# A selective scan and a quantized layer on eight cores: four of a tile's 16 states, in place of three, go without DMA transposes

## The chip, the cores and the metric

The program runs on the 8 cores of one Trainium2 chip. The input has 4 sequences of 2048 positions and 4096 channels. Core c takes one half (1024 positions) of sequence c // 2. The cores exchange nothing: a core that has a second half works out for itself the state in which the first half ends. All cores run the same instructions. The metric is the device time of the slowest core in microseconds (us), lower is better; the time given is the median over runs.

## The reference

With D = 4096 channels, N = 16 states for each channel, and C, B and dt computed from x:

```python
A = -exp(A_log)
xp = einsum('bld,rd->blr', x, x_proj_w)           # gives dt_in (128), B (16), C (16)
dt = softplus(einsum('blr,dr->bld', dt_in, dt_proj_w) + dt_proj_b)
h[t] = exp(dt[t] * A) * h[t-1] + dt[t] * B[t] * x[t]   # for each channel and each of 16 states
y[t] = sum_n(h[t, n] * C[t, n]) + D * x[t]
x = layernorm(x + y)
x = layernorm(x + ffn(x))    # ffn: 4096 x 4096, rows and weights rounded to 8 bits, product rescaled
```

## The kernel before

It has three stages. First the projection of x to dt_in, B and C. Then the scan, in 32 tiles of 128 channels with 16 states each, which are 512 states `g`; the change is here. Last the quantized layer and the second normalization. `L981` and the like are lines of the kernel; PE is TensorE, DVE is VectorE, ACT is ScalarE, POOL is GpSimd, SP is SyncE, whose queue issues the transfers of the scan.

**The scan of one state.** Channels lie on partitions, 1024 positions on the free axis. ACT makes the decay `dAr` (L727). PE makes the input `ps_I` (L505): the transposed `uT` (dt times x) against a diagonal matrix of B, 8 matmuls. DVE scans `hr = dAr * h + ps_I` (L981). Then C must be multiplied in and the 16 states summed into `ps_y`. An ordinary state does it through a DMA transpose: SP turns `hr` to `hT` (L340, `turn_h`), and PE multiplies a diagonal matrix of C by `hT` (L539). A state in `ZN` does it without: POOL multiplies `hr` by a replicated C (`gz`, L1199, `times_C`), and PE adds it in with an identity matrix (L530).

**The state that is carried in.** The first half of the sequence (the prefix) gives only its last state. ACT makes decays `Er` of it (L718). An ordinary state: POOL weighs `wr = Er * up` (L1188, `weigh`), SP turns it to `wT` (L334, `turn_w`), PE sums against a column of B into `ps_c` (L469). DVE copies the finished sums of the whole tile to `carry` in one instruction (L960, `take_carry`), which the scans of the next tile wait for. A state in `ZN`: PE multiplies the transposed `upT` by a diagonal matrix into one of the two `ps_I` buffers (L492), and DVE multiplies and sums it with the decay `Ez` in one instruction (L947, `last_state_z`). So it needs neither `wr` nor `wT`.

**The order.** Every engine's order is written out. All loop over g; the part of the loop with g % 16 = n is called slot n here. In slot n

- DVE does `last_state_z` if the state 18 ahead is in `ZN` (before the change in slots 2, 7 and 12), then the scan of state n; after slot 8's scan the reversed sum of dt (L915, its first operand is `ones`), after slot 10's scan `dD` (L953), after slot 13's scan `take_carry`;
- ACT makes the decay `dAr` for 3 states ahead, once the scan of the slot before is over, then `Er` or `Ez` for 21 states ahead, then pieces of dt;
- POOL does `times_C` if state n - 1 is in `ZN`, then `weigh` for 21 states ahead (nothing if that one is in `ZN`), and at the end of slot 4 `up` (L1167), of slot 6 `uo` (L1174), of slot 7 the cast of x (L1179);
- SP issues `turn_w` for 21 states ahead, which waits for POOL, then `turn_h` for state n, and behind these `yT_st` and `xp` in slot 6, `upT` in slot 7, `uT` in slot 8, `xo` in slot 9;
- PE fills `ps_I` for slot n + 1 (the prefix group first, if that slot has one), then sums `ps_c` for 18 states ahead, then adds states into `ps_y`, most of them three slots after their scan; states 0 and 1 are added in slot 5, behind the evacuation of the tile before (L734).

The last state of a tile that goes into `carry`, number 15, is weighed and turned in slot 10. Ring sizes: `hr` 5, `hT` 6, `wr` 4, `wT` 5, `ps_I` 2, `Er` 3, `Ez` 2, `gz` 2. A scan waits until the state five before it has been turned or multiplied by C.

Of the kernel before, what the change touches and what calls it, by code (L numbers as in the profile page):

```python
# [8 lines left out]
BF16 = mybir.dt.bfloat16  # L9
# [9 lines left out]
def _build(D, P, L, N, R):  # L19
# [10 lines left out]
    nc = bass.Bass("TRN2", target_bir_lowering=False)  # L30
# [16 lines left out]

    c_hbm = nc.dram_tensor("c_st", [3, L], BF16).ap()
    yT_hbm = nc.dram_tensor("yT_st", [L, D], BF16).ap()
# [4 lines left out]
    with es:  # L54
# [88 lines left out]
        esD = ExitStack()  # L143
        BT = sb(esD, "BT", 2 * NC8 * 32, BF16)
        diagB = sb(esD, "diagB", N * NC8 * 128, BF16)
        diagC = sb(esD, "diagC", N * NC8 * 128, BF16)
        ones = sb(esD, "ones", P, BF16)
        xp, xo = sb(esD, "xp", P), sb(esD, "xo", L)
# [6 lines left out]
        uo = sb(esD, "uo", L, BF16)  # L155
        Crep = sb(esD, "Crep", 3 * L, BF16)
        gz = [sb(esD, f"gz{k}", L, BF16) for k in range(2)]
# [10 lines left out]
        carry = sb(esD, "carry", 2 * N)  # L168
        carryZ = sb(esD, "carryZ", 2 * 3)
        yTs = sb(esD, "yTs", 2 * L, BF16)  # L170
# [42 lines left out]
        def nz(k):  # L213

            return 3 * (k // N) + sum(1 for z in ZN if z < k % N)

# [49 lines left out]
        def _(sp):  # L266
# [39 lines left out]

            sp.wait_ge(l_cst, 48)
            sp.dma_start(out=Crep[:], in_=bass.AP(c_hbm.tensor, 0, [[0, 128], [1, 3 * L]])).then_inc(l_C, 16)

# [10 lines left out]
            def turn_up(i):  # L320
                sp.wait_ge(g_up, i + 1)
                if i >= 2:
                    sp.wait_ge(p_P, 3 * (i - 1))
                sp.dma_start(out=by_piece(upT[i % 2]), in_=up[i % 2][:], transpose=True).then_inc(l_up, 16)
# [559 lines left out]
        def _(v):  # L884
# [26 lines left out]
            def reverse_sum(i):  # L911

                v.wait_ge(a_ln, 2 * i + 1)
                v.wait_ge(g_up, i + 1)
                nc.vector.tensor_tensor_scan(dtp[i % 2][:], ones[:], dtp[i % 2][:], tot[i % 2][:],  # L915
                                             OP.mult, OP.subtract).then_inc(v_R, 1)
# [22 lines left out]
            def last_state_z(p):  # L939
                i, n = divmod(p, N)  # L940
                o = (i % 2) * 3 + ZN.index(n)
                v.wait_ge(a_E, p + 1)
                v.wait_ge(p_P, nz(p) + 1)
                if i >= 2:
                    v.wait_ge(v_O, N * (i - 2) + n + 1)
                E = Ez[nz(p) % 2]
                nc.vector.scalar_tensor_tensor(E[:], E[:], 1.0, ps_I[place[("P", p)] % 2][:],  # L947
                                               OP.mult, OP.mult, accum_out=carryZ[:, o : o + 1]).then_inc(v_P, 1)
# [13 lines left out]
            def scan(g):  # L962
# [191 lines left out]
        def _(g_):  # L1154
# [35 lines left out]
            def times_C(g):  # L1190
# [125 lines left out]
```

## Time and profile before

| | |
|---|---|
| three runs | 2585.11, 2590.03, 2603.1 us; median 2590.03 |
| profiled execution | 2607.06 us in all; span of its slowest core 2605.5 us |
| spans of the 8 cores | 2585.2 to 2605.5 us |
| first scan to last scan in the profile | about 202 to 1832 us |
| busy share of the span | DVE 72%, PE 63%, ACT 62%, POOL 54% |

The trace is of the slowest core in one execution. In its timelines each row is a start, a duration, the engine, the line, the operation, the tiles, a count, and in brackets how long the engine was idle before it and what it then got. An "x2" stands for two instructions in a row. Instructions that follow each other directly overlap a little in these rows, so two scans take 4.58 us and not twice 2.33. A row of an SP issue is the time that the queue took for it, not the transfer; how long it takes until data lands is in the table of issues. The DMA share of a stretch is a mean over 16 engines and can exceed 1.

### The profile page before, as it was taken

The numbers are of one execution on the slowest core, as the hardware profiler recorded it, in microseconds if no ns is written. First come the engines' busy times: TensorE is split into PE (matmuls) and PEld (weight loads), VectorE is DVE, ScalarE is ACT, GpSimd is POOL, SyncE is SP. The second block draws the span as 40 slices with busy tenths as digits, with TensorE's granted clock in tenths as the row PEclk, the third lists the DMA queues.
The fourth block names the chain that finished last, engine by engine and source line by source line (L and its number), as shares of the span: only waits on it lengthen the run. The fifth ranks groups of instructions, "written<-read, shape, count | busy, mean of one in ns | idle before, by whom it ended". The sixth has DMA issues, their size and how long they took to land.

```text
span 2605.5 us, 47762 instructions; the slowest of 8 cores (2585.2 to 2605.5 us)
## 1 busy us (share of the span) xinstructions
PE 1641.3 (63%) x16180; PEld 1242.0 (48%) x16304; DVE 1885.6 (72%) x1375; ACT 1611.1 (62%) x1603; POOL 1395.0 (54%) x733
## 2 busy tenths in 40 slices
PE   4615566666666656666666656566134579999993
PEld 1114555555555555655555555556023345555541
DVE  1188888888888988888888888889464545555543
ACT  2356777787777777877787777776255444444420
POOL 0027788778877877887788778874112101111110
PEclk8956666666666666666666666767557789999997
DMA  9868999999998999999999999998877445656559
GB/s 312 283 121 139 166 158 174 172 165 164 185 172 155 176 168 172 156 177 172 164 163 173 179 165 157 180 172 134 267 283 246 184 155 201 201 195 202 195 205 339
DMA packets 1014787, 491.47 MB, mean 189 GB/s; under 512 B 984723, under 2 KB 984851, under 8 KB 1000982
## 3 DMA queue, kind: packets, MB, share of 16 engines
q1 hardware_dynamic: 998326, 360.48, 72.6%
q10 hardware_dynamic: 5472, 79.69, 8.7%
q0 software_dynamic: 10752, 48.24, 5.6%
q8 instruction: 136, 2.23, 0.4%
q14 instruction: 101, 0.83, 0.2%
HBM read 196.77 MB, written 56.63 MB: 97 GB/s over the span
## 4 chain that ended last, share of the span: by engine, by line
PE 23%; SPq 22%; DMA 17%; DVE 14%; issue 10%; POOL 8%; ACT 5%; another core or an unknown queue 1%; DVEq 0%; ACTq 0%; POOLq 0%
PE ps_F L615 15%; SPq L340 10%; DVE hr L981 8%; SPq L334 8%; DMA hT<-hr 5%; POOL wr L1188 4%; DMA xld<-xT 4%; DMA ye<-yT_st 4%; PE ps_y L539 2%; PE ps_T L598 2%; POOL up L1167 2%; DMA wT<-wr 2%; PE ps_I L505 2%; ACT Er L718 2%; POOL gz L1199 1%
## 5 line engine op out<-in xcount | busy, mean ns | idle before, releaser
L1188 POOL TENSOR_TENSOR wr<-Er,up 128x1024 bf16<-128x1024 bf16 x399 | 855.4, 2147 | 340.4 <-ACT Er L718 328.5
L981 DVE TENSOR_TENSOR_SCAN hr<-dAr,carry,ps_I 128x1024 bf16<-128x1024 bf16 x416 | 960.1, 2332 | 65.8 <-PE ps_I L505 63.8
L727 ACT ACTIVATE dAr<-dto,A_sb 128x1024 bf16<-128x1024 f32 x512 | 585.7, 1145 | 371.6 <-DVE hr L981 367.3
L505 PE MATMUL ps_I<-diagB,uT 128*128 128x128 bf16 x4096 | 439.7, 271 | 230.8 <-DVE hr L981 223.3
L539 PE MATMUL ps_y<-hT,diagC 128*128 128x128 bf16 x3328 | 354.9, 277 | 224.3 <-DMA hT<-hr 224.0
L505 PEld LDWEIGHTS ps_I<-diagB,uT 128*128 128x128 bf16 x4096 | 357.1, 125 | 266.8 <-issue 264.6
L718 ACT ACTIVATE Er<-dtp,A_sb 128x1024 bf16<-128x1024 f32 x416 | 471.5, 1135 | 15.6 <-DVE wr L937 9.3
L615 PE MATMUL ps_F<-slab,xqT 128*128 128x512 bf16 x1989 | 452.0, 382 | 5.0 <-issue 1.1
L539 PEld LDWEIGHTS ps_y<-hT,diagC 128*128 128x128 bf16 x3328 | 285.2, 126 | 244.1 <-issue 243.7
L615 PEld LDWEIGHTS ps_F<-slab,xqT 128*128 128x128 bf16 x2048 | 200.4, 99 | 234.6 <-issue 9.8
L469 PE MATMUL ps_c<-BT,wT 128*128 128x1 bf16 x3328 | 146.1, 166 | 170.8 <-DMA wT<-wr 150.6
L469 PEld LDWEIGHTS ps_c<-BT,wT 128*128 128x128 bf16 x3328 | 136.5, 105 | 198.3 <-issue 197.1
L1199 POOL TENSOR_TENSOR gz<-hr,Crep 128x1024 bf16<-128x1024 bf16 x96 | 203.9, 2124 | 50.0 <-DVE hr L981 49.7
L981 DVE TENSOR_TENSOR_SCAN hr<-dAr,carryZ,ps_I 128x1024 bf16<-128x1024 bf16 x96 | 223.4, 2327 | 4.4 <-issue 0.5
L1068 DVE SCALAR_TENSOR_TENSOR o<-ps_F,asc,wscR 128x512 f16<-128x512 f32 x64 | 48.0, 751 | 209.7 <-PE ps_F L615 209.6
L1234 POOL DMA_DIRECT2D dch<-d_st x64 | 35.3, 551 | 299.3 <-DMA r_st<-dch 205.6
L825 ACT ACTIVATE sqj<-dch 128x512 bf16<-128x512 f32 x56 | 35.3, 630 | 253.1 <-DVE dch L1082 253.1
L947 DVE SCALAR_TENSOR_TENSOR Ez<-Ez,ps_I 128x1024 bf16<-128x1024 bf16 x96 | 116.8, 1217 | 100.9 <-PE ps_I L492 100.6
L1036 DVE TENSOR_REDUCE wamax<-Wn 128x1 f32<-128x4096 f32 x32 | 141.1, 4410 | 2.0 <-DMA Wn<-W 2.0
L1167 POOL TENSOR_TENSOR up<-dtp,xp 128x1024 bf16<-128x1024 f32 x32 | 75.9, 2371 | 112.4 <-DMA xp<-xT 101.3
L587 PE MATMUL ps_T<-identh_sb,qb 128*128 128x128 f16 x256 | 29.4, 302 | 143.7 <-ACT qb L781 91.1
L788 ACT ACTIVATE qb<-Wn,wqs 128x4096 f16<-128x4096 f32 x32 | 118.3, 3698 | 0.0
(94 smaller groups left out, 1899.9 us busy)
## 6 DMA issues: line engine op xcount, KB each, us to landing
Wn<-W ACTq DMA_DIRECT2D x30, 2048.0 KB, 9.6
xld<-xT SPq DMA_DIRECT2D x32, 1024.0 KB, 11.3
xp<-xT SPq DMA_DIRECT2D x32, 512.0 KB, 5.5
xo<-xT SPq DMA_DIRECT2D x32, 512.0 KB, 5.1
slab<-x_own SPq DMA_DIRECT2D x8, 2048.0 KB, 12.2
d_st<-slab POOLq DMA_DIRECT2D x8, 2048.0 KB, 13.3
dch<-d_st POOLq DMA_DIRECT2D x64, 256.0 KB, 3.6
r_st<-dch POOLq DMA_DIRECT2D x56, 256.0 KB, 3.7
```

Of the source, the lines that this page charges most:

```text
L334: sp.dma_start(out=by_piece(wT[k % 5]), in_=wr[k % 4][:], transpose=True).then_inc(l_w[k % 5], 16)
L340: sp.dma_start(out=by_piece(hT[g % 6]), in_=hr[g % 5][:], transpose=True).then_inc(l_h[g % 6], 16)
L469: mm = pe.matmul(ps_c[:, o : o + 1], wT[k % 5][:, c * 128 : (c + 1) * 128], BT[:, c * 32 + n : c * 32 + n + 1], start=(c == 0), stop=(c == ...
L505: mm = pe.matmul(ps[:, c * 128 : (c + 1) * 128], uT[i % 2][:, c * 128 : (c + 1) * 128], diagB[:, o : o + 128], start=True, stop=True)
L539: mm = pe.matmul(ps_y[:, c * 128 : (c + 1) * 128], diagC[:, o : o + 128], hT[g % 6][:, c * 128 : (c + 1) * 128], start=False, stop=(n == N ...
L615: mm = pe.matmul(ps_F[q % 5][:], xqT[:, kt * L + tt * 128 : kt * L + (tt + 1) * 128], slab[jg % 2][:, kt * 512 : (kt + 1) * 512], start=(k ...
L718: act.activation(dst[:], dtp[i % 2][:], AF.Exp, scale=A_sb[:, p : p + 1]).then_inc(a_E, 1)
L727: act.activation(dAr[g % 4][:], dto[i % 3][:], AF.Exp, scale=A_sb[:, g : g + 1]).then_inc(a_dA, 1)
L981: nc.vector.tensor_tensor_scan(hr[g % 5][:], dAr[g % 4][:], ps_I[place[("O", g)] % 2][:], first, OP.mult, OP.add).then_inc(v_O, 1)
L1036: v.reduce_max(wamax[:, b : b + 1], Wn[b % 2][:], axis=AX.X, apply_absolute_value=True).then_inc(v_wam, 1)
L1188: g_.tensor_tensor(wr[k % 4][:], Er[k % 3][:], up[i % 2][:], OP.mult).then_inc(g_w, 1)
L1199: g_.tensor_tensor(gz[z % 2][:], hr[g % 5][:], Crep[:, o : o + L], OP.mult).then_inc(g_c, 1)
```

## The change

States 2, 6, 10 and 14 of each tile go the way without transposes, in place of 4, 9 and 14. For room in SBUF `ones` shrinks from 1024 columns to 16, and the reversed sum reads its first element with a step of 0.

```diff
-    c_hbm = nc.dram_tensor("c_st", [3, L], BF16).ap()
+    c_hbm = nc.dram_tensor("c_st", [4, L], BF16).ap()
...
-        ones = sb(esD, "ones", P, BF16)
+        ones = sb(esD, "ones", 16, BF16)
...
-        Crep = sb(esD, "Crep", 3 * L, BF16)
+        Crep = sb(esD, "Crep", 4 * L, BF16)
...
-        carryZ = sb(esD, "carryZ", 2 * 3)
+        carryZ = sb(esD, "carryZ", 2 * 4)
...
-        ZN = (4, 9, 14)
+        ZN = (2, 6, 10, 14)
...
-            return 3 * (k // N) + sum(1 for z in ZN if z < k % N)
+            return 4 * (k // N) + sum(1 for z in ZN if z < k % N)
...
-            sp.wait_ge(l_cst, 48)
-            sp.dma_start(out=Crep[:], in_=bass.AP(c_hbm.tensor, 0, [[0, 128], [1, 3 * L]])).then_inc(l_C, 16)
+            sp.wait_ge(l_cst, 64)
+            sp.dma_start(out=Crep[:], in_=bass.AP(c_hbm.tensor, 0, [[0, 128], [1, 4 * L]])).then_inc(l_C, 16)
...
-                nc.vector.tensor_tensor_scan(dtp[i % 2][:], ones[:], dtp[i % 2][:], tot[i % 2][:],
+                nc.vector.tensor_tensor_scan(dtp[i % 2][:], bass.AP(ones, 0, [[16, 128], [0, P]]), dtp[i % 2][:], tot[i % 2][:],
...
-            for it in diag_order[:3]:
+            for it in diag_order[:4]:
...
-            left = diag_order[3:]
+            left = diag_order[4:]
...
-                    g_.wait_ge(p_y, (z - 2) // 3 * N + ZN[(z - 2) % 3] + 1)
+                    g_.wait_ge(p_y, (z - 2) // 4 * N + ZN[(z - 2) % 4] + 1)
...
-                o = (z % 3) * L
+                o = (z % 4) * L
```


In each tile there are two transposes fewer (12 `wT`, 12 `hT`, `upT` and `uT`, where there were 13 and 13), one `weigh` fewer and one `times_C` more on POOL, and one more L947 on DVE. `last_state_z` now stands in slots 0, 4, 8 and 12; slots 1, 5, 9 and 13 have no `wr` and no `wT`, slots 2, 6, 10 and 14 no `hT`.

SP's queue from the `wT` of slot 6 to that of slot 10, before (ahead of it stand `wT` and `hT` of slot 5):

```order
L334 DMA_TRANSPOSE wT<-wr 128x8x128
L340 DMA_TRANSPOSE hT<-hr 128x8x128
L344 DMA yT_st<-yTs 128x8x128
L297 DMA xp<-xT 128x1024
L334 DMA_TRANSPOSE wT<-wr 128x8x128
L340 DMA_TRANSPOSE hT<-hr 128x8x128
L324 DMA_TRANSPOSE upT<-up 128x8x128
L334 DMA_TRANSPOSE wT<-wr 128x8x128
L340 DMA_TRANSPOSE hT<-hr 128x8x128
L318 DMA_TRANSPOSE uT<-uo 128x8x128
L302 DMA xo<-xT 128x1024
L334 DMA_TRANSPOSE wT<-wr 128x8x128
```

The same changed, from the `wT` of slot 6 (ahead of it stands the `hT` of slot 5, which has no `wT` now) to those of slots 10 and 11:

```order
L334 DMA_TRANSPOSE wT<-wr 128x8x128
L344 DMA yT_st<-yTs 128x8x128
L297 DMA xp<-xT 128x1024
L334 DMA_TRANSPOSE wT<-wr 128x8x128
L340 DMA_TRANSPOSE hT<-hr 128x8x128
L324 DMA_TRANSPOSE upT<-up 128x8x128
L334 DMA_TRANSPOSE wT<-wr 128x8x128
L340 DMA_TRANSPOSE hT<-hr 128x8x128
L318 DMA_TRANSPOSE uT<-uo 128x8x128
L340 DMA_TRANSPOSE hT<-hr 128x8x128
L302 DMA xo<-xT 128x1024
L334 DMA_TRANSPOSE wT<-wr 128x8x128 x2
```

Slot 6 has no `hT` any more, slot 9 has one, and between the `wT` of slot 7 and that of slot 10 there stand 7 transfers where there were 6.

POOL in slots 4 to 8 before (the first row is slot 4's `up`; its four rows with `wr` belong to slots 5, 6, 7 and 8):

```order
L1167 TENSOR_TENSOR up1<-dtp1,xp 128x1024
L1199 TENSOR_TENSOR gz1<-hr0,Crep 128x1024
L1188 TENSOR_TENSOR wr2<-Er1,up0 128x1024
L1188 TENSOR_TENSOR wr3<-Er2,up0 128x1024
L1174 TENSOR_TENSOR uo<-dto2,xo 128x1024
L1188 TENSOR_TENSOR wr0<-Er0,up0 128x1024
L1179 CAST x160<-xo 128x1024
L1188 TENSOR_TENSOR wr1<-Er1,up0 128x1024
```

The same changed, from slot 3's `gz` to slot 8's `wr`:

```order
L1199 TENSOR_TENSOR gz0<-hr3,Crep 128x1024
L1188 TENSOR_TENSOR wr2<-Er0,up0 128x1024
L1188 TENSOR_TENSOR wr3<-Er1,up0 128x1024
L1167 TENSOR_TENSOR up1<-dtp1,xp 128x1024
L1188 TENSOR_TENSOR wr0<-Er2,up0 128x1024
L1174 TENSOR_TENSOR uo<-dto2,xo 128x1024
L1199 TENSOR_TENSOR gz1<-hr2,Crep 128x1024
L1188 TENSOR_TENSOR wr1<-Er0,up0 128x1024
L1179 CAST x160<-xo 128x1024
L1188 TENSOR_TENSOR wr2<-Er1,up0 128x1024
```

`gz` moved out of slot 5 into slots 3 and 7, and slot 4 has a `wr`, in front of `up`. In slot 7 a `gz` stands ahead of the `wr`.

DVE from slot 12 (its L947) to slot 2 of the next tile, before; the row L960 is `take_carry`:

```order
L947 SCALAR_TENSOR_TENSOR Ez0,carryZ<-Ez0,ps_I0 128x1024
L981 SCALAR_TENSOR_TENSOR hr3<-dAr0,carry,ps_I1 128x1024
L981 SCALAR_TENSOR_TENSOR hr4<-dAr1,carry,ps_I0 128x1024
L960 COPY carry<-ps_c 128x16
L981 SCALAR_TENSOR_TENSOR hr0<-dAr2,carryZ,ps_I1 128x1024
L981 SCALAR_TENSOR_TENSOR hr1<-dAr3,carry,ps_I0 128x1024
L981 SCALAR_TENSOR_TENSOR hr2<-dAr0,carry,ps_I1 128x1024
L981 SCALAR_TENSOR_TENSOR hr3<-dAr1,carry,ps_I0 128x1024
L947 SCALAR_TENSOR_TENSOR Ez1,carryZ<-Ez1,ps_I1 128x1024
```

The same changed, from slot 12 to slot 1:

```order
L947 SCALAR_TENSOR_TENSOR Ez1,carryZ<-Ez1,ps_I1 128x1024
L981 SCALAR_TENSOR_TENSOR hr3<-dAr0,carry,ps_I0 128x1024
L981 SCALAR_TENSOR_TENSOR hr4<-dAr1,carry,ps_I1 128x1024
L960 COPY carry<-ps_c 128x16
L981 SCALAR_TENSOR_TENSOR hr0<-dAr2,carryZ,ps_I0 128x1024
L981 SCALAR_TENSOR_TENSOR hr1<-dAr3,carry,ps_I1 128x1024
L947 SCALAR_TENSOR_TENSOR Ez0,carryZ<-Ez0,ps_I0 128x1024
L981 SCALAR_TENSOR_TENSOR hr2<-dAr0,carry,ps_I1 128x1024
L981 SCALAR_TENSOR_TENSOR hr3<-dAr1,carry,ps_I0 128x1024
```

Behind `take_carry` the L947 of slot 2 now stands two scans earlier, in slot 0.

## Rows read from the trace of the kernel before

**Rows 1.** The page: span and cores, transfer rate in 40 slices, HBM traffic.

```profile
span 2605.5 us, 47762 instructions; the slowest of 8 cores (2585.2 to 2605.5 us)
...
GB/s 312 283 121 139 166 158 174 172 165 164 185 172 155 176 168 172 156 177 172 164 163 173 179 165 157 180 172 134 267 283 246 184 155 201 201 195 202 195 205 339
...
HBM read 196.77 MB, written 56.63 MB: 97 GB/s over the span
```

**Rows 2.** Busy time by stretch: the 30 middle tiles, then 4.5 us inside one.

```profile
core 2: us, PE busy (x) PEld busy (x) DVE busy (x) ACT busy (x) POOL busy (x), PEclk, DMA share, GB/s
210.50:1761.40 1550.90, 960.43 (x11819) 870.94 (x11878) 1324.69 (x751) 1186.94 (x1197) 1238.63 (x571) 0.66 1.00 168
1049.00:1053.50 4.50, 4.50 (x42) 4.22 (x41) 2.61 (x2) 4.50 (x6) 4.36 (x4) 0.50 0.46 88
```

**Rows 3.** Waits of VectorE over the same 30 tiles: total us, times, longest.

```profile
engine line waited for: us in total, times, longest us
DVE Ez L947 <- PE ps_I L492: 98.8, 70, 3.4
DVE hr L981 <- PE ps_I L505: 63.6, 85, 3.1
DVE carry L960 <- PE ps_c L469: 57.5, 30, 3.7
```

**Rows 4.** Timeline of VectorE over one tile and into the next.

```profile
1039.81 4.58 DVE L981 TENSOR_TENSOR_SCAN hr<-dAr,carry,ps_I 128x1024 bf16<-128x1024 bf16 x2
...
1052.99 1.22 DVE L947 SCALAR_TENSOR_TENSOR Ez<-Ez,ps_I 128x1024 bf16<-128x1024 bf16 x1 [1.89 <-PE ps_I L492]
...
1069.92 1.22 DVE L947 SCALAR_TENSOR_TENSOR Ez<-Ez,ps_I 128x1024 bf16<-128x1024 bf16 x1 [0.55 <-PE ps_I L492]
...
1074.18 2.35 DVE L981 TENSOR_TENSOR_SCAN hr<-dAr,carry,ps_I 128x1024 bf16<-128x1024 bf16 x1 [0.77 <-PE ps_I L505]
1078.11 0.17 DVE L960 COPY carry<-ps_c 128x16 f32<-128x16 f32 x1 [1.58 <-PE ps_c L469]
...
1085.18 4.58 DVE L981 TENSOR_TENSOR_SCAN hr<-dAr,carry,ps_I 128x1024 bf16<-128x1024 bf16 x2 [2.17 <-PE ps_I L505]
1090.33 1.22 DVE L947 SCALAR_TENSOR_TENSOR Ez<-Ez,ps_I 128x1024 bf16<-128x1024 bf16 x1 [0.57 <-PE ps_I L492]
...
1091.47 4.58 DVE L981 TENSOR_TENSOR_SCAN hr<-dAr,carry,ps_I 128x1024 bf16<-128x1024 bf16 x2
```

**Rows 5.** Timeline of SP's queue in the same tile: the issues of transfers.

```profile
1053.38 1.23 SPq L334 DMA_TRANSPOSE wT<-wr  x1
...
1059.76 1.92 SPq L297 DMA_DIRECT2D xp<-xT  x1
1061.84 1.25 SPq L334 DMA_TRANSPOSE wT<-wr  x1
...
1071.43 0.52 SPq L302 DMA_DIRECT2D xo<-xT  x1
1072.11 1.24 SPq L334 DMA_TRANSPOSE wT<-wr  x1
```

**Rows 6.** Timeline of GpSimd in the same tile.

```profile
1044.64 2.12 POOL L1188 TENSOR_TENSOR wr<-Er,up 128x1024 bf16<-128x1024 bf16 x1 [1.77 <-ACT Er L718]
1046.72 2.36 POOL L1167 TENSOR_TENSOR up<-dtp,xp 128x1024 bf16<-128x1024 f32 x1
...
1055.47 2.37 POOL L1174 TENSOR_TENSOR uo<-dto,xo 128x1024 bf16<-128x1024 f32 x1
1057.79 2.13 POOL L1188 TENSOR_TENSOR wr<-Er,up 128x1024 bf16<-128x1024 bf16 x1
```

**Rows 7.** Timeline of ScalarE there: slot 4's and slot 6's prefix decay.

```profile
1046.42 1.13 ACT L718 ACTIVATE Ez<-dtp,A_sb 128x1024 bf16<-128x1024 f32 x1
...
1052.05 1.14 ACT L718 ACTIVATE Er<-dtp,A_sb 128x1024 bf16<-128x1024 f32 x1
```

**Rows 8.** Timeline of TensorE there: three groups that had waited.

```profile
1048.81 1.01 PE L525 MATMUL ps_y<-dD,x 128*128 128x128 bf16 x8 [0.84 <-ACT yTs L734]
...
1077.60 0.34 PE L469 MATMUL ps_c<-BT,wT 128*128 128x1 bf16 x8 [2.15 <-DMA wT<-wr]
...
1083.07 1.01 PE L539 MATMUL ps_y<-hT,diagC 128*128 128x128 bf16 x8 [2.59 <-DMA hT<-hr]
```

**Rows 9.** Issues of transposes: count and median us from issue to landing.

```profile
hT<-hr SPq DMA_TRANSPOSE x416, 3.4
```

More of the change, by code:

```diff
@@ L322, in turn_up @@
                 if i >= 2:
-                    sp.wait_ge(p_P, 3 * (i - 1))
+                    sp.wait_ge(p_P, 4 * (i - 1))
                 sp.dma_start(out=by_piece(upT[i % 2]), in_=up[i % 2][:], transpose=True).then_inc(l_up, 16)
@@ L940, in last_state_z @@
                 i, n = divmod(p, N)
-                o = (i % 2) * 3 + ZN.index(n)
+                o = (i % 2) * 4 + ZN.index(n)
                 v.wait_ge(a_E, p + 1)
@@ L973, in scan @@
                     v.wait_ge(v_P, nz(g) + 1)
-                    o = (i % 2) * 3 + ZN.index(n)
+                    o = (i % 2) * 4 + ZN.index(n)
                     first = carryZ[:, o : o + 1]
```

## The prediction

> **What bounds the kernel now.** The scan takes 1630 of 2605 us, and the change touches nothing else but the memsets and loads ahead of it. I read first the busy time by stretch [rows 2]: over 30 tiles (1550.9 us, so 51.7 us a tile) DVE is busy 1324.7 us, 85%, and the DMA share is 1.00, while PE, ACT and POOL have 62 to 80%. So two candidates are near their limit. Next the waits of DVE in those tiles [rows 3]: 219.9 us, 7.3 a tile, none of them on DMA by name: 98.8 for the prefix group of PE, 63.6 for the input group, 57.5 for the carry sums. Who makes PE late is seen in one tile of typical length [rows 4]. The scans of slots 2 and 3 start at 1039.81 and take 4.58 together, so slot 2's ends at 1042.10, which I call 0; in the next tile the same point is 1091.47 + 2.29 = 1093.76, or 51.66. DVE waits 1.89 before the L947 of slot 7, 0.55 before that of slot 12, 0.77 at slot 13, 1.58 for the carry, 2.17 at slot 0 and 0.57 before the L947 of slot 2: 7.53 in all, near the mean.
>
> Behind these stands one loop. The carry copy (at 36.01) comes 0.51 after PE's last group for it, which had waited 2.15 for a `wT` [rows 8]; that is the `wT` which SP issued for slot 10 at 1072.11 [rows 5]. The reader is to see that this transfer took 5.4 us to reach PE, where the median landing is 3.4 [rows 9]: it stood in a queue. The queue formed from slot 5's `wT` on (issued at 11.28; before that a hole, with a DMA share of 0.46 in 1049 to 1053.5 [rows 2], while SP waited for POOL). **Price of one transpose:** from 1053.38 to 1077.60 are 24.2 us, which hold 10 transposes ahead of the last, 1.31 MB of plain transfers (`yT_st`, `xp`, `xo`) and one landing of 3.4. At 312 GB/s, the rate of the first slice, where plain loads run [rows 1], the plain ones take 4.2 us; so (24.2 - 3.4 - 4.2) / 10 = 1.66 us each. After the carry the same queue holds back the `hT` of slot 11: PE waits 2.59 for it until 1083.07 [rows 8], and only behind it fills the input of slot 0, for which DVE waits 2.17.
>
> **The change, part by part.**
>
> *DVE.* One more L947, 1.14 from start to the next start [rows 4] (1090.33 to 1091.47); its own work is certain. From 0 to the end of slot 13's scan (1074.18 + 2.35 = 34.43) there are 3.21 us of waits and so 31.2 of work; with L947 in slots 4, 8 and 12 in place of 7 and 12 it is 32.4.
>
> *Slots 7 and 8.* The 1.89 before slot 7's L947 comes from PE's slot 5, where `ps_y` waits 0.84 for the evacuation [rows 8] and three groups for `ps_y` follow. Without L947 in slot 7 its scan meets the same late PE: the fill would be ready about 1 to 1.5 us too late, and the prefix group for slot 8 comes behind two sums, some 0.6 more. The extra L947 in slot 4 gives ACT time to end the evacuation. I keep 1.9 for both, bounds 0.5 and 3.
>
> *POOL, the hole, and the leg to the carry.* POOL's sum hardly changes (a `gz` of 2.1 for a `wr` of 2.1), but its order does. Slot 3's `wr` ends at 4.7 as now [rows 6]. Slot 4's prefix decay is ready at 1046.42 + 1.13 = 5.45 [rows 7], its new `wr` ends at 7.6, `up` (2.3) at 9.9. Slot 6's decay is ready at 11.1 [rows 7]: `wr` to 13.2, `uo` to 15.5, `gz` to 17.6, slot 7's `wr` to 19.7. Now SP issues that `wT` at 1061.84, which is 19.7 too [rows 5], but behind a full queue (the issue of `xp` took 1.92); in the changed kernel `wT` of slot 6, `yT_st` and `xp` are long done and the queue is empty. From 19.7 to the carry's `wT` there stand 7 transposes and `xo` (0.52 MB, 1.7 us): 19.7 + 7 x 1.66 + 1.7 + 3.4 = 36.4, and the copy 0.5 later, at **36.9 against 36.0**. DVE itself would be there at 32.4 + 3.2 = 35.6, so the transfer still ends last and covers the added L947. Bounds: 35.6, if the light queue moves at the 1.4 us in which SP issues transposes, and 38.3, if slot 8's `wr`, behind a cast, is 1.4 late as well.
>
> *From the carry on.* From 1078.11 to 1093.76 are 15.65 us, with 2.74 of waits, so 12.9 of work; L947 only moves from slot 2 to slot 0. In the queue behind slot 10's `wT` the `hT` of slots 10 and 14 and the `wT` of slot 13 are gone, the `wT` of slot 15 is new: at slot 1 two transposes fewer. The `hT` of slot 11 is served at 34.7 + 2 x 1.66 = 38.0 and lands at 39.7. The same count for the kernel before gives 40.4, and the row says 41.0, so I add 0.6: 40.3. PE then needs a group for `ps_y` and the prefix group (1 us each) and has it ready at 42.2; slot 15's scan ends at 36.9 + 0.3 + 4.5 = 41.7. The wait is 0.5, and later `hT` fit. I take 0.6 in place of 2.74; bounds 0 and 2.74, all of it.
>
> *The sum* is 36.9 + 12.9 + 0.6 = 50.4 against 51.66, that is 1.26 less a tile and **38 us less over 30 tiles**. The last tile has no prefix work and stays. Ahead of the loop DVE gains one L947 and loses one weighing and most of the memset of `ones`, and `Crep` loads 0.26 MB more while DVE works on the first tile: taken as 0, bounds 3 either way. The step of 0 on `ones` I take as 0: L915 has time to spare ahead of the carry, where a gain is swallowed. The profiled run's 2607.1 us would become 2569; it lies 17 above the median of the runs, so the forecast is 2590 - 38 = **2552 us**.
>
> **The rivals.**
>
> *DVE is the bound, and each L947 is paid in full.* For it: 85% busy, and every prefix group now costs DVE 98.8 / 90 = 1.1 us of waiting beside its 1.14. Against it: the carry copy waits in 30 of 30 tiles, so DVE has slack there. The place is slots 15 to 1, where the prefix group now stands ahead of slot 0's fill on a PE at half clock (0.50 in a stretch of [rows 2], a group of 8 in 1.0 us). If its waits there are PE's own order and not the queue, they stay at 2.74, and the tile takes 36.9 + 12.9 + 2.74 = 52.5: 26 us more, 2616; with the L947 also paid before the carry (another 0.4) 2629. It decides from 1.9 us of waits after the carry. The Trainium skill, page Perfetto Trace Analysis, section Identifying the Most-Contended Engine, says to take the engine with the highest occupancy as the one that limits, and to judge DMA not by occupancy but by its HBM use; HBM moves only 97 GB/s here [rows 1], so by that rule DVE is the bound and this case holds. The waits of PE on `wT` and `hT` [rows 8] speak against the rule here. Chance 0.20.
>
> *Gain and loss cancel.* POOL comes later to slot 7's `wr` than I have it, the hole grows, and the carry comes at 38.1 in place of 36.9. Then 51.6 a tile: 2590. Chance 0.22.
>
> *The transfers bound all of it.* The share of 1.00 speaks for it, the hole of each tile against. Then two transposes of 1.66 leave each tile: 3.3 x 30 = 100 us, 2490. Chance 0.06.
>
> **How the numbers follow.** The forecast has 0.52. About 1% (26 us) is what a measurement of this kernel can tell from no change. The forecast's own range is 2516 to 2579: no waits after the carry and the carry half of its possible 1.3 earlier (49.2 a tile), or the carry 0.9 later (51.3). The range reaches over the second rival and into the first: **2515 to 2618**. Faster by over 1%: 0.45 of the forecast and the last rival, 0.51. Within 1%: the rest of the forecast, 0.20 of the cancelling case and 0.03 of the first rival, 0.30. Slower: 0.19.
>
> **What would show it.** In the changed profile: L947 x128; transposes `wT` and `hT` x384 each; POOL's `wr` of slot 7 ending 19.7 after slot 2's scan; the carry copy at about 36.9 and still waiting for `wT`; less than 1 us of waits after it; the tile at 50.4. Wrong would be a carry without a wait (DVE bound), waits in slots 15 to 1 that end with PE while PE does not wait for `hT`, or a hole in the transfers of slots 5 to 7 of more than 3 us that pushes the carry beyond 38.

## The result: slower by 2.1%, outside the range

| | before | changed |
|---|---|---|
| runs, us | 2585.11 to 2603.1, median 2590.42 (4) | 2647.09 to 2649.12, median 2648.01 (4) |
| ratio | 1 | 1.0213 [1.0182, 1.0244] |
| profiled execution, us | 2607.06 | 2648.1 |

The forecast was 2552, the range ended at 2618, and "slower" had 0.19. The measured time is 58 us above the kernel before. Here and below, medians are over all executions and ratios, with a 95% interval, over the undisturbed ones alone, since in some executions the cores of half the chip ran some per cent slower: where they disagree, the ratio counts. The change has the fewer transposes that it was to have, and the tile still grew.

The page of the changed kernel: its span (before: [rows 1]), SyncE's transfer queue (packets, MB, share of 16 engines' span) and the transposes of `hr` (before: [rows 9]).

```profile
span 2646.5 us, 47917 instructions; the slowest of 8 cores (2624.8 to 2646.5 us)
...
q1 hardware_dynamic: 930744, 343.96, 62.6%
...
hT<-hr SPq DMA_TRANSPOSE x384, 2.8
```

384 transposes, as forecast, and as many of `wr`. They also land in 2.8 us where it was 3.4; that was not forecast (last section). Busy time by stretch, in the columns of [rows 2]: first the 30 middle tiles, then 6 us inside one tile.

```profile
205.80:1798.60 1592.80, 960.38 (x11885) 846.39 (x11882) 1350.27 (x812) 1181.58 (x1199) 1234.82 (x570) 0.68 0.84 154
1074.00:1080.00 6.00, 1.39 (x24) 1.17 (x24) 6.00 (x3) 2.60 (x3) 6.00 (x3) 0.80 0.50 124
```

1592.8 us for 30 tiles are 53.1 a tile, where 51.7 were before. Every engine's work is about what it was, TensorE's granted clock is 0.68 where it was 0.66, and the mean share of the DMA engines fell from 1.00 to 0.84. The waits of DVE over those tiles, in the columns of [rows 3]:

```profile
DVE carry L960 <- PE ps_c L469: 114.1, 30, 5.2
DVE hr L981 <- PE ps_I L505: 75.8, 73, 2.6
DVE Ez L947 <- PE ps_I L492: 45.1, 40, 2.8
```

The wait for the carry doubled, 57.5 to 114.1. The one before L947 halved, the one before scans grew by 12. So the loss is in the carry, which is where the forecast put its risk; the question is what makes its last `wT` late. One tile of the changed kernel, first DVE; slot 2's scan ends at 1054.65 + 2.32 = 1056.97, which is 0 here:

```profile
1054.65 2.32 DVE L981 TENSOR_TENSOR_SCAN hr<-dAr,carryZ,ps_I 128x1024 bf16<-128x1024 bf16 x1
...
1073.79 3.94 DVE L915 TENSOR_TENSOR_SCAN dtp<-ones,tot,dtp 128x1024 f32<-128x1024 bf16 x1
...
1096.45 0.17 DVE L960 COPY carry<-ps_c 128x16 f32<-128x16 f32 x1 [3.91 <-PE ps_c L469]
...
1107.25 2.32 DVE L981 TENSOR_TENSOR_SCAN hr<-dAr,carryZ,ps_I 128x1024 bf16<-128x1024 bf16 x1
```

The carry is at 39.5, after a wait of 3.91 (36.0 and 1.58 in [rows 4]), and the tile ends at 1109.57, 52.6. GpSimd in the same tile, slots 2 and then 6 to 8:

```profile
1057.62 2.12 POOL L1188 TENSOR_TENSOR wr<-Er,up 128x1024 bf16<-128x1024 bf16 x1 [3.91 <-ACT Er L718]
...
1069.04 2.13 POOL L1188 TENSOR_TENSOR wr<-Er,up 128x1024 bf16<-128x1024 bf16 x1 [0.71 <-ACT Er L718]
1071.12 2.37 POOL L1174 TENSOR_TENSOR uo<-dto,xo 128x1024 bf16<-128x1024 f32 x1
1073.45 2.13 POOL L1199 TENSOR_TENSOR gz<-hr,Crep 128x1024 bf16<-128x1024 bf16 x1
1075.53 4.10 POOL L1188 TENSOR_TENSOR wr<-Er,up 128x1024 bf16<-128x1024 bf16 x1
1079.58 1.03 POOL L1179 CAST x<-xo 128x1024 bf16<-128x1024 f32 x1
```

The row that matters is the one at 1075.53. It is slot 7's `wr`, the same operation on the same shapes as its neighbours with 2.12, and it takes 4.10. It ends at 22.7 (1079.63), where the forecast had 19.7. SP's queue waits for it:

```profile
1071.29 1.22 SPq L334 DMA_TRANSPOSE wT<-wr  x1
...
1073.23 0.52 SPq L297 DMA_DIRECT2D xp<-xT  x1
1079.77 1.22 SPq L334 DMA_TRANSPOSE wT<-wr  x1
...
1089.94 4.70 SPq L334 DMA_TRANSPOSE wT<-wr  x2
```

From 1073.75 to 1079.77 SP issues nothing. Before the change the hole stood ahead of slot 5's `wT` (1053.38 in [rows 5]) and lasted 2.6 us; now it stands behind slot 6 and lasts 6.0, with a DMA share of 0.50. The `wT` of slots 10 and 11 follow from 1089.94, and PE waits for the one of slot 10:

```profile
1095.92 0.35 PE L469 MATMUL ps_c<-BT,wT 128*128 128x1 bf16 x8 [3.15 <-DMA wT<-wr]
```

Over 28 tiles of the slowest core the means are (offsets from the end of slot 2's scan, us; one profiled execution each, "cast" and L915 are medians over the kernel):

| kernel | slot 7 `wr` ends | L915 | cast | carry copy | tile |
|---|---|---|---|---|---|
| before | 17.8 | 3.44 | 3.04 | 36.4 | 51.8 |
| changed | 22.7 | 3.43 | 1.03 | 39.9 | 53.1 |

### The profile page after: what moved, and what is told of

It is laid out like the page before. It is cut to its first block, busy times and chain, and to the rows that moved or that the text cites. A ratio compares the mean times of both kernels' runs of the same rounds, so it can differ in the third digit from the quotient of the medians.

```text
span 2646.5 us, 47917 instructions; the slowest of 8 cores (2624.8 to 2646.5 us)
## 1 busy us (share of the span) xinstructions
PE 1649.8 (62%) x16304; PEld 1220.2 (46%) x16304; DVE 1911.5 (72%) x1438; ACT 1605.8 (61%) x1603; POOL 1383.8 (52%) x734
## 4 chain that ended last, share of the span: by engine, by line
PE 25%; DMA 17%; issue 15%; ACT 13%; SPq 12%; DVE 10%; POOL 8%; ACTq 0%; DVEq 0%; POOLq 0%
PE ps_F L615 15%; POOL wr L1188 6%; DMA wT<-wr 5%; DVE hr L981 5%; SPq L340 4%; SPq L334 4%; DMA ye<-yT_st 4%; DMA xld<-xT 4%; ACT dAr L727 3%; PE ps_I L505 3%; ACT Er L718 3%; PE ps_T L598 2%; ACT Ez L718 2%; PE ps_y L539 2%; DMA hT<-hr 2%
## 5 line engine op out<-in xcount | busy, mean ns | idle before, releaser
L1188 POOL TENSOR_TENSOR wr<-Er,up 128x1024 bf16<-128x1024 bf16 x368 | 836.8, 2284 | 349.5 <-ACT Er L718 341.8
L981 DVE TENSOR_TENSOR_SCAN hr<-dAr,carry,ps_I 128x1024 bf16<-128x1024 bf16 x384 | 889.8, 2334 | 79.3 <-PE ps_I L505 78.0
L718 ACT ACTIVATE Er<-dtp,A_sb 128x1024 bf16<-128x1024 f32 x384 | 435.5, 1135 | 14.6 <-DVE wr L937 8.5
L539 PE MATMUL ps_y<-hT,diagC 128*128 128x128 bf16 x3072 | 327.5, 275 | 148.6 <-DMA hT<-hr 147.6
L539 PEld LDWEIGHTS ps_y<-hT,diagC 128*128 128x128 bf16 x3072 | 263.5, 126 | 170.2 <-issue 168.1
L1199 POOL TENSOR_TENSOR gz<-hr,Crep 128x1024 bf16<-128x1024 bf16 x128 | 272.0, 2125 | 96.6 <-DVE hr L981 96.6
L981 DVE TENSOR_TENSOR_SCAN hr<-dAr,carryZ,ps_I 128x1024 bf16<-128x1024 bf16 x128 | 297.8, 2326 | 4.6 <-issue 0.5
L947 DVE SCALAR_TENSOR_TENSOR Ez<-Ez,ps_I 128x1024 bf16<-128x1024 bf16 x128 | 154.6, 1208 | 48.1 <-PE ps_I L492 46.3
L718 ACT ACTIVATE Ez<-dtp,A_sb 128x1024 bf16<-128x1024 f32 x128 | 145.2, 1134 | 0.0
L492 PE MATMUL ps_I<-diagC,upT 128*128 128x128 bf16 x1024 | 107.3, 267 | 24.6 <-DVE Ez L947 15.1
## 6 DMA issues: line engine op xcount, KB each, us to landing
slab<-x_own SPq DMA_DIRECT2D x8, 2048.0 KB, 12.9
d_st<-slab POOLq DMA_DIRECT2D x8, 2048.0 KB, 13.9
```

What stands on the lines that cost most here:

```text
L492: mm = pe.matmul(ps[:, c * 128 : (c + 1) * 128], upT[i % 2][:, c * 128 : (c + 1) * 128], diagC[:, o : o + 128], start=True, stop=True)
L539: mm = pe.matmul(ps_y[:, c * 128 : (c + 1) * 128], diagC[:, o : o + 128], hT[g % 6][:, c * 128 : (c + 1) * 128], start=False, stop=(n == N ...
L718: act.activation(dst[:], dtp[i % 2][:], AF.Exp, scale=A_sb[:, p : p + 1]).then_inc(a_E, 1)
L981: nc.vector.tensor_tensor_scan(hr[g % 5][:], dAr[g % 4][:], ps_I[place[("O", g)] % 2][:], first, OP.mult, OP.add).then_inc(v_O, 1)
L1188: g_.tensor_tensor(wr[k % 4][:], Er[k % 3][:], up[i % 2][:], OP.mult).then_inc(g_w, 1)
```

## The theories

**P**: slot 7's `wr` on GpSimd comes late, because it and L915 on DVE exclude each other; the hole in the transfers and the late carry follow from it. **D**: VectorE is the bound, and each added L947 is paid (the first rival of the prediction).

P rests on the durations of L915, the cast (L1179) and slot 7's `wr`. The summaries of the first two, with count, min/median/max ns, first and last start, in the kernel before:

```profile
L915 DVE TENSOR_TENSOR_SCAN dtp<-ones,tot,dtp x32: 2340/3439/4343, 141.6 to 1729.4; 128x1024 f32<-128x1024 bf16 x32
...
L1179 POOL CAST x<-xo x32: 1032/3037/3054, 157.7 to 1777.7; 128x1024 bf16<-128x1024 f32 x32
```

and the changed kernel:

```profile
L915 DVE TENSOR_TENSOR_SCAN dtp<-ones,tot,dtp x32: 2324/3434/4347, 137.8 to 1764.4; 128x1024 f32<-128x1024 bf16 x32
...
L1179 POOL CAST x<-xo x32: 1027/1031/1044, 153.9 to 1817.6; 128x1024 bf16<-128x1024 f32 x32
```

L915 needs 2.33 us when nothing is in its way, the cast 1.03. In the tile above GpSimd's `gz` began at 1073.45; L915 was issued at 1073.79 and "takes" 3.94: it stands until `gz` ends at 1075.58 and then works 2.2. GpSimd's `wr` was issued at 1075.53 and "takes" 4.10: it stands until L915 ends at 1077.73 and then works 1.9. Before the change the same thing fell on the cast:

```profile
1057.79 2.13 POOL L1188 TENSOR_TENSOR wr<-Er,up 128x1024 bf16<-128x1024 bf16 x1
1058.63 3.44 DVE L915 TENSOR_TENSOR_SCAN dtp<-ones,tot,dtp 128x1024 f32<-128x1024 bf16 x1
1059.86 3.05 POOL L1179 CAST x<-xo 128x1024 bf16<-128x1024 f32 x1
```

L915 stands until `wr` ends at 1059.92, and the cast until L915 ends at 1062.07. No other engine waits for the cast, and slot 8's `wr` behind it was early enough all the same (a run below tests this), so 2 us were lost for nothing there; now they fall on the one `wr` for which the queue, PE and the carry wait. The other scans read one of their inputs from PSUM and keep their 2.31 to 2.35 beside any GpSimd work. The Trainium skill states this (page SBUF — State Buffer, section Who interferes with whom): a DVE instruction with two inputs in SBUF and a GpSimd instruction that reads SBUF contend for one shared port pair, whoever issues first has it for the whole instruction, and the other is blocked entirely. The traces agree, down to who is first: L915 was issued 0.34 us after `gz` and is held by it, and `wr` 1.74 us after L915 and is held by that.

## The experiments

**The small `ones` alone**, on the kernel before. Where nothing else is said, edits are against the changed kernel. Each ratio is against the kernel before, executed alongside, whose median was 2589 to 2596 us; so a difference of two medians can be some us off. Where a line is added, the lines behind it have numbers one higher (L916 for L915).

```diff
-        ones = sb(esD, "ones", P, BF16)
+        ones = sb(esD, "ones", 16, BF16)
...
-                nc.vector.tensor_tensor_scan(dtp[i % 2][:], ones[:], dtp[i % 2][:], tot[i % 2][:],
+                nc.vector.tensor_tensor_scan(dtp[i % 2][:], bass.AP(ones, 0, [[16, 128], [0, P]]), dtp[i % 2][:], tot[i % 2][:],
```

> The kernel before with one part of the change alone: `ones` has 16 columns and the reversed sum (L915) reads it with a step of 0. Both theories (P: GpSimd's `wr` of slot 7 comes late; D: VectorE is the bound and each added L947 is paid) put none of the loss here: 2590, within 0.5%, L915 at a median of 3.4 us as before. A rival that the step of 0 costs something expects L915 above 3.6 us or the time over 2600.

Measured 2578.22, ratio 0.9947 [0.9925, 0.997]: a small gain, tile 50.6, carry 35.7. The step of 0 costs nothing (L915 3.47, cast 3.04). So the part of the change that makes room is a gain of some 0.5%, and what the new places and the fourth state cost must be counted from 2578: 70 us, not 58.

**A stand-in with one input from SBUF for the reversed sum.** The kernel leaves the reversed sum out, so its decays, and with them its output, are not the layer's; it serves for the timing alone.

```diff
+        rjunk = sb(esD, "rjunk", 3)
...
-                nc.vector.tensor_tensor_scan(dtp[i % 2][:], bass.AP(ones, 0, [[16, 128], [0, P]]), dtp[i % 2][:], tot[i % 2][:],
-                                             OP.mult, OP.subtract).then_inc(v_R, 1)
+                v.reduce_max(rjunk[:], bass.AP(dtp[i % 2], 0, [[P, 128], [0, 3], [1, P]]), axis=AX.X).then_inc(v_R, 1)
```

> The changed kernel with the reversed sum of dt left out and in its place, on the same engine and of nearly the same length, a reduce_max over 3 x 1024 columns (about 3.3 us), which reads one SBUF input and not two. P, with the cause that the two-input L915 and GpSimd exclude each other: slot 7's `wr` takes 2.1 us and not 4.1, ends at 20.6 after slot 2's scan and not at 22.7, the carry copy comes at about 38 and not 39.9, 51.1 us a tile, 2588. D: VectorE has as much to do as before, so 2648 or at most 4 less.

Measured 2593.15, ratio 1.0023 [1.0008, 1.0038]: below the changed kernel by 55 us as the medians go, by 49 as the ratios go. The stand-in holds DVE for 3.33 us, about as long as L915 did, and reads one input from SBUF; `wr` beside it is as short as ever. DVE and GpSimd in one tile, whose 0 is 1019.31:

```profile
1035.61 2.12 POOL L1199 TENSOR_TENSOR gz<-hr,Crep 128x1024 bf16<-128x1024 bf16 x1
1036.44 3.33 DVE L916 TENSOR_REDUCE rjunk<-dtp 128x3 f32<-128x3072 f32 x1
1037.70 2.12 POOL L1188 TENSOR_TENSOR wr<-Er,up 128x1024 bf16<-128x1024 bf16 x1
...
1056.33 0.18 DVE L960 COPY carry<-ps_c 128x16 f32<-128x16 f32 x1 [3.61 <-PE ps_c L470]
```

On the mean slot 7's `wr` ends at 20.7, the carry comes at 38.1 and the tile takes 51.2: 2.0 us of `wr` less give 1.9 us of tile. That is the test of P: DVE is busy there for as long as before, and what is gone is the second input and with it the exclusion. D gives no reason for the gain.

**The same stand-in in the kernel before**, with the small `ones` (edit as the two above together).

> The twin of the reduce_max run on the kernel before (with the small `ones`, 2578 by itself): the reversed sum left out, in its place a reduce_max of the same length with one SBUF input. P: GpSimd's cast falls from 3.0 to 1.0 us, as in the changed kernel, but here the cast takes the exclusion and the transfers behind it are not late, so nothing is gained: 2568 to 2582, while the same edit gave the changed kernel 55. A rival by which the exclusion costs its 2 us a tile wherever it falls expects 2578 - 60 = 2518.

Measured 2581.34, ratio 0.9944 [0.9923, 0.9964], the same as the small `ones` alone, although the cast fell from 3.04 to 1.04 us. Slot 8's `wr`, behind the cast, ends at 20.8 in place of 22.8, and the carry is no earlier for it (36.3). So the exclusion cost nothing where it fell before the change, and the gain of the run above is no gift of the stand-in.

**L915 two scans later**, where the changed kernel's GpSimd is not at slot 7's `wr`.

```diff
-                if n == 8 and i + 2 < NT:
+                if n == 10 and i + 2 < NT:
```

> The changed kernel with the reversed sum moved from behind slot 8's scan to behind slot 10's. P: slot 7's `wr` is free of it and ends at 20.6; it now meets the `wr` of slot 8 or 10, which have 1 to 4 us to spare; carry at about 38, 51.1 us a tile, 2588. D: the same work in another order, 2648.

Measured 2599.26, ratio 1.003 [1.0001, 1.0059], 49 us below the changed kernel with nothing left out. `wr` ends at 20.7 again, the carry comes at 37.9, the tile is 51.1: P without any stand-in. In the profiled execution the 11 us above the expected 2588 do not lie in the scan. From its first scan to its last it takes 1610.8 us, 63 less than the changed kernel (1673.9), and the part behind the last scan takes 787 where the changed kernel's took 774; over the profiled executions of all kernels here, whose code is the same in that part, it is 773 to 787 (787 with 6, 10 and 14 as well). The move isn't free either: L915 now has a median of 3.93 us and once 7.81, and ScalarE waits for it before slot 11's prefix decay (79 us in 30 tiles, none in the changed kernel).

**`wr` ahead of `gz` in slot 7.**

```diff
-                if g >= 1 and is_z(g - 1):
+                late = n == 7
+                if g >= 1 and is_z(g - 1) and not late:
...
+                if g >= 1 and is_z(g - 1) and late:
+                    times_C(g - 1)
```

> The changed kernel with one pair exchanged on GpSimd: in slot 7 `wr` stands ahead of the `gz` of state 6. P with exclusion: `wr` is asked for at about 17.5, when L915 (from 16.8, now not held up by `gz`, so 2.3 us long) is running; it runs from 19.1 to 21.2, 1.5 us earlier than now, and so the carry: 2648 - 45 = 2603. P without exclusion (the 4.1 us are a slower `wr`): 2.1 us earlier, 2585. D: no change, 2648.

Measured 2607.89, ratio 1.0085 [1.0054, 1.0116]. The time is near, the way to it another. GpSimd and DVE in one tile (0 is 1034.09):

```profile
1050.38 2.12 POOL L1188 TENSOR_TENSOR wr<-Er,up 128x1024 bf16<-128x1024 bf16 x1
1051.22 3.44 DVE L915 TENSOR_TENSOR_SCAN dtp<-ones,tot,dtp 128x1024 f32<-128x1024 bf16 x1
1052.46 4.10 POOL L1199 TENSOR_TENSOR gz<-hr,Crep 128x1024 bf16<-128x1024 bf16 x1
```

`wr` is first and ends at 18.4, four us sooner than in the changed kernel, and `gz` takes the 4.10. Behind it slot 8's `wr` ends at 25.7, as late as in the changed kernel, and the carry is at 38.4. Four us at slot 7 gave 1.5 us at the carry; the next run shows that slot 8's `wr` is the next bound.

**Both, L915 later and `wr` first.** (Edit: the two above.)

> The changed kernel with both edits: the reversed sum behind slot 10's scan, and `wr` ahead of `gz` in GpSimd's slot 7. P: `wr` of slot 7 ends at 18.6, of slot 8 at 23.8 (25.7 with the exchange alone, which is what then held the carry at 38.4); from there 4 transposes, `xo`, a landing and the copy: 36.0 to 36.5 for the carry, 13.2 from it on, 49.5 a tile: 2540, 50 less than the kernel before. D: 2648.

Measured 2569.85, ratio 0.9882 [0.9846, 0.9918]: faster than before the change, but 20 to 30 us short of what I expected. GpSimd and DVE in one tile (0 is 1015.24):

```profile
1031.57 2.13 POOL L1188 TENSOR_TENSOR wr<-Er,up 128x1024 bf16<-128x1024 bf16 x1
...
1035.72 1.05 POOL L1179 CAST x<-xo 128x1024 bf16<-128x1024 f32 x1
1036.14 2.77 DVE L915 TENSOR_TENSOR_SCAN dtp<-ones,tot,dtp 128x1024 f32<-128x1024 bf16 x1
1036.71 6.19 POOL L1188 TENSOR_TENSOR wr<-Er,up 128x1024 bf16<-128x1024 bf16 x2
1038.83 2.05 DVE L953 TENSOR_SCALAR dD<-identb_sb,dvec_sb 128x128 bf16<-128x128 bf16 x1
```

Slot 7's `wr` ends at 18.5. But behind slot 10's scan L915 meets the two `wr` of slots 8 and 9: together they take 6.19 where two take 4.20, and `dD` (L953) takes 2.05, which is 0.62 in the changed kernel. Which of the two `wr` is held changes from tile to tile, and that shows what it is worth: in 10 of 29 tiles, this one among them, it is slot 8's, which ends at 25.7, with the carry at 38.5 and a tile of 51.7; in the other 19 slot 8's ends at 23.8, with the carry at 37.1 and a tile of 50.2. The mean carry is 37.6.

**Three such states at 6, 10 and 14**, on the kernel before, to part the places from the number.

```diff
-        ZN = (4, 9, 14)
+        ZN = (6, 10, 14)
```

> The kernel before with its three states moved to 6, 10 and 14, so that three of the changed kernel's four places are there and the fourth state, its L947 and its two transposes fewer are not: placement alone. P: slot 7's `wr` is as late as in the changed kernel (22.7), since `gz` of state 6 and L915 both stand in its way; carry at 39.9; from it on 11.8 of work and 0.5 to 1.5 of waits: 52.2 to 53.2 a tile, 2610 to 2640. D (the fourth L947 is the loss): 2590.

Measured 2630.5, ratio 1.0105 [1.0054, 1.0155], 27 us more than before as the ratio goes. GpSimd and DVE in one tile:

```profile
1050.05 3.16 DVE L915 TENSOR_TENSOR_SCAN dtp<-ones,tot,dtp 128x1024 f32<-128x1024 bf16 x1
1051.03 4.10 POOL L1188 TENSOR_TENSOR wr<-Er,up 128x1024 bf16<-128x1024 bf16 x1
```

With three of them and only the places of the changed kernel the same `wr` takes 4.10 and the kernel is 1% slower; it ends at 22.3, the carry comes at 39.3 and the tile takes 52.0, each 0.2 to 0.6 below what was expected. No fourth L947 is in it, so D can't explain it.

**A useless 1.1 us on DVE in each tile**, on the kernel before with the small `ones`.

```diff
+        rjunk = sb(esD, "rjunk", 1)
...
+                if n == 4:
+                    v.reduce_max(rjunk[:], diagB[:, 0:L], axis=AX.X)
```

> The kernel before with the small `ones` (2578 by itself) and one useless instruction of about 1.1 us on VectorE ahead of slot 4's scan, a reduce_max with one SBUF input, which costs VectorE what an added L947 costs and nothing else. P: it is covered by the wait for the carry (1.6 to 1.9 a tile): 2578 to 2587. D: 1.1 x 31 = 34 more, 2612.

Measured 2585.13, ratio 0.9955 [0.9931, 0.9978], against 0.9947 without the extra work: 2 us more by the ratios, 7 by the medians, where D asks for 34. Ahead of the carry DVE has slack, though it is busy 85% of the time before the change [rows 2]. (Behind the carry no such work was tried.)

**Other places for the four states**: 4, 9 and 14 as before, and 12 for the fourth.

```diff
-        ZN = (2, 6, 10, 14)
+        ZN = (4, 9, 12, 14)
```

> The changed kernel with the four states placed as 4, 9, 12, 14: the kernel before's three and state 12, so that GpSimd's slots 4 to 8 stay as they were before, except that slot 7 has no `wr` at all, and L915 meets the cast again. P (the loss is GpSimd's late `wr` in slots 6 and 7, a matter of placement and not of four states): the leg to the carry starts at 11.2 as before and holds 9 transposes and 1.31 MB, one transpose less, so the carry comes at 35 to 36, and less is in the queue after it: 49.5 to 50.3 us a tile, 2530 to 2550. D (each added L947 is paid): 2590 + 39 = 2629 or more.

Measured 2531.63, ratio 0.974 [0.9699, 0.9781]; **measured again**, with an expectation of its own:

> The changed kernel with states 4, 9, 12, 14 once more, in five rounds: 2532, a ratio of 0.974 to the kernel before and 0.956 to the changed one's 2648.

2544.61, ratio 0.9795 [0.9776, 0.9815], 12 us above that expectation; the two intervals only just meet. So four states do gain, 2.0 to 2.6%, with the same number of L947, `gz`, `wr` and transposes as the changed kernel. State 12 is the one that slot 7 would weigh: there is no `wr` in that slot. The summaries of L915 and the cast, and the waits of DVE from 205.8 to 1745:

```profile
L915 DVE TENSOR_TENSOR_SCAN dtp<-ones,tot,dtp x32: 2325/2346/4341, 140.0 to 1648.8; 128x1024 f32<-128x1024 bf16 x32
...
L1179 POOL CAST x<-xo x32: 1026/1039/1057, 156.1 to 1694.2; 128x1024 bf16<-128x1024 f32 x32
```

```profile
DVE Ez L947 <- PE ps_I L492: 67.4, 41, 3.9
...
DVE carry L960 <- PE ps_c L469: 22.9, 23, 2.5
```

L915 comes behind the cast here and has 2.35 us, the cast 1.04. The exclusion isn't gone: in each of the 28 tiles slot 8's `wr`, behind the cast, waits for L915. GpSimd in one tile:

```profile
1009.11 1.04 POOL L1179 CAST x<-xo 128x1024 bf16<-128x1024 f32 x1
1010.41 3.80 POOL L1188 TENSOR_TENSOR wr<-Er,up 128x1024 bf16<-128x1024 bf16 x1 [0.25 <-ACT Er L718]
```

But with no `wr` in slot 7 it ends at 20.8 all the same (22.8 before, 25.7 in the changed kernel). The carry comes at 34.8, and the waits for it fall to 22.9 us in all. The tile is 49.2.

**The freed columns given back as an unused tile**, behind the small `ones` on the kernel before.

```diff
         ones = sb(esD, "ones", 16, BF16)
+        pad = sb(esD, "pad", P - 16, BF16)
```

> The kernel before with the small `ones` and, right behind it, an unused tensor that fills the rest of its old place, so that every other tensor lies where it lay before. It asks why the transposes land in 2.9 us with the small `ones` and in 3.4 with the full one. If the places of the tensors decide: 3.4 again, 2590. If the step of 0 decides: 2.9 and 2578.

Measured 2595.47, ratio 1.0003 [0.9986, 1.002]: the gain of the small `ones` is gone, with every instruction the same. See the last section.

**All kernels side by side**, from the end of slot 2's scan, means of 28 tiles, us; the step of the prediction that failed is the first column.

| kernel | slot 7 `wr` ends | slot 8 `wr` ends | carry copy | tile | ratio |
|---|---|---|---|---|---|
| before | 17.8 | 22.8 | 36.4 | 51.8 | 1 |
| before, small `ones` | 17.8 | 22.8 | 35.7 | 50.6 | 0.9947 |
| the same with the unused tile | 17.8 | 22.8 | 35.7 | 51.1 | 1.0003 |
| small `ones` and stand-in for L915 | 17.8 | 20.8 | 36.3 | 51.2 | 0.9944 |
| small `ones` and useless 1.1 us | 17.8 | 22.8 | 36.2 | 50.9 | 0.9955 |
| three states: 6, 10, 14 | 22.3 | 25.4 | 39.3 | 52.0 | 1.0105 |
| changed | 22.7 | 25.7 | 39.9 | 53.1 | 1.0213 |
| changed, stand-in for L915 | 20.7 | 23.7 | 38.1 | 51.2 | 1.0023 |
| changed, L915 two scans later | 20.7 | 24.0 | 37.9 | 51.1 | 1.003 |
| changed, `wr` first | 18.6 | 25.7 | 38.4 | 51.5 | 1.0085 |
| changed, both | 18.6 | 24.4 | 37.6 | 50.8 | 0.9882 |
| four states: 4, 9, 12, 14 | none | 20.8 | 34.8 | 49.2 | 0.974 |

Each row is one profiled execution, which can lie some 10 us (0.3 a tile) or more off its kernel's median: "before" and "unused tile" are equally fast by their ratio and differ by 0.7 in carry and tile. In the kernels with the states 2, 6, 10 and 14 the carry comes 17.2 to 17.4 behind slot 7's `wr` where that ends at 20.7 or later, and 12.7 to 13.2 behind slot 8's where slot 7's ends at 18.6. In those that keep 4, 9 and 14 the queue was already full, and 2 us less at slot 8's `wr` (the stand-in) moved nothing.

## Why the prediction was wrong

**The loop that bounds: right.** The `wT` that ends the carry, the queue ahead of it and the hole ahead of the queue were the right chain. The leg from the end of slot 7's `wr` to the carry was forecast at 36.9 - 19.7 = 17.2 and measures 39.93 - 22.68 = 17.25. Not each part was right, though: the median landing of a `wT` is now 2.8 us and not 3.4, so the 7 transposes and `xo` must have taken as much more than their 13.3. That the two cancel is luck. (The 5.4 us in which the `wT` of slot 10 reached PE before the change are 1077.60 - 1072.11 = 5.5; nothing hangs on it.)

**After the carry: right.** 12.9 + 0.6 = 13.5 was forecast, 53.1 - 39.9 = 13.2 is measured (15.4 before). That is 2.2 us a tile of gain. Some 0.5 of it belongs to the small `ones` and not to the fewer transposes (14.9 with that alone), a gain that the forecast put at 0. The first rival had its loss in this place, and there is none.

**DVE: right.** L947 x128; ahead of the carry DVE still has slack, as its wait of 3.91 for the carry and the useless 1.1 us show.

**"Slot 7's `wr` to 19.7": this step failed**, by 3.0 us (22.7), and it carries the whole miss.

One us of it is ScalarE. I took "slot 6's decay is ready at 11.1" from [rows 7] as if ScalarE's work did not move. With L947 gone from slot 2 the scans of slots 1 and 2 follow each other closer than ScalarE's work for them. At 0 it still has slot 2's work, starts slot 3's at 1057.90, which is 0.93 (0.15 before: it had waited 0.63 for that scan), and runs without a gap to slot 6's decay. That start before the change:

```profile
1042.25 1.15 ACT L727 ACTIVATE dAr<-dto,A_sb 128x1024 bf16<-128x1024 f32 x1 [0.63 <-DVE hr L981]
```

and after it, with slot 6's decay:

```profile
1057.90 1.14 ACT L727 ACTIVATE dAr<-dto,A_sb 128x1024 bf16<-128x1024 f32 x1
...
1067.70 1.14 ACT L718 ACTIVATE Er<-dtp,A_sb 128x1024 bf16<-128x1024 f32 x1
```

It is ready at 1068.84, 11.9, and GpSimd's `wr` of slot 6 starts 0.2 later and ends at 14.2 in place of 13.2. That moves `uo`, `gz` and `wr` alike: 20.7, as the two kernels without the exclusion there have it. The other kernels fit: slot 6's `wr` ends at 13.4 on the mean in all kernels that have an L947 in slot 2 (those with state 4), at 14.2 in the five with 2, 6, 10 and 14, and at 13.9 with 6, 10 and 14.

The other 2.0 are the exclusion. It stood in the trace of before, as 3.05 us for a cast. I used that row as the cast's own price (for the bound "slot 8's `wr` ... 1.4 late") and did not ask why a cast of the same size as `up` should take longer than `up` with 2.36. L915 was costed as "has time to spare ahead of the carry", which is true of DVE and beside the point: its price was on GpSimd.

The sum with the measured terms: 50.4 + 1.0 + 2.0 - 0.3 = 53.1, which is the measured mean. Against [rows 2] that is 1.4 a tile, 42 us in 30 tiles, and the profiled runs differ by 41. The medians differ by 58, since the profiled run of before lay 17 above its median. The kernel with the unused tile, of the same speed as before, has a profiled run of 2589.4 and 51.1 a tile, so (53.1 - 51.1) x 30 = 60.

**The small `ones` at 0: wrong too, the other way.** They gave 12 us (2578 for 2590, ratio 0.9947), which are inside the measured 2648. Without them the miss would have been larger.

**The rivals.** The second one ("POOL comes later to slot 7's `wr`, the hole grows") had the mechanism, and stopped at a carry of 38.1 because nothing in it was priced beyond lateness by order; it came at 39.9. The last section of the prediction names what happened: "a hole in the transfers of slots 5 to 7 of more than 3 us that pushes the carry beyond 38". The first rival had the sign and, with 2616 to 2629, the nearer number, by a cause that the runs refute.

**Open:** whether the longer part behind the last scan (787 us) belongs to the kernel with L915 two scans later or to that one execution; and how much of the gain of 4, 9, 12, 14 is the missing `wr` in slot 7, and how much the order of the queue. No run parts these.

## What to carry to other kernels

A duration in a trace can hold a wait that no view calls one: when an instruction takes longer than its shape's other rows or than its own minimum, find what runs beside it before its row is used as a price, and ask on whom that wait will fall when the order moves. If an order is changed at one place, the ready times of every other engine in the leg are worked out anew, not read from the old trace. With work that may stand anywhere, the place mattered more than the amount: four such states cost 2.1% at 2, 6, 10 and 14 and gave 2.0 to 2.6% at 4, 9, 12 and 14.

## What the runs showed of the hardware

Where tensors lie in SBUF changes how fast DMA transposes run. With `ones` at 1024 columns, or at 16 and an unused tile of the rest behind it, `hT` has a median landing of 3.3 to 3.4 us (three kernels); with 16 columns alone, of 2.8 to 2.9 (three kernels). All six have the same 416 transposes of `hr`, of the same shapes. The queue's and the transposes' rows, first with the unused tile:

```profile
q1 hardware_dynamic: 998326, 360.48, 73.0%
...
hT<-hr SPq DMA_TRANSPOSE x416, 3.4
```

and with the small `ones` alone:

```profile
q1 hardware_dynamic: 998326, 360.48, 68.0%
...
hT<-hr SPq DMA_TRANSPOSE x416, 2.9
```

The same 998326 packets take 73.0% and 68.0% of the engines' span. It is worth 0.5% of this kernel's time. Which property of an address does it was not tried. This gain is inside the change and hid part of its loss.

The exclusion is not a slowdown by sharing: a held row is the time until the other engine's instruction ends, plus the free duration, less 0.2 us. In the tile of the changed kernel `wr` has 2.20 + 2.12 - 0.2 = 4.1 (4.10 measured) and L915 has 1.79 + 2.33 - 0.2 = 3.9 (3.94 measured). In the kernel before, the changed one, the one with `wr` first and the one with 6, 10 and 14 each such pair in the middle tiles keeps this within 0.03 us, whether the held GpSimd instruction is the cast, `wr` or `gz`. A reduction with one input from SBUF (L916, 3.33 us) beside GpSimd's `wr` left it at 2.12, but `dD`, one small matrix times a column, took 2.05 us beside it in the kernel with both edits (median of 32; 0.24 at the least). The Trainium skill says in the same section (page SBUF — State Buffer, Who interferes with whom) that a `tensor_scalar` whose operands allow it can run in a two-port mode, and can then contend as well. The row agrees as to the contention; in which mode `dD` ran no run here shows.
